# Graph attention edge stage: the gathers leave out rows of the neighbouring node tile

## What is computed

```python
dst = sorted destinations; src = their sources          # 106250 each, 6250 of them self loops
xh    = (layernorm(x) @ W).reshape(N, 8, 32)
a_src, a_dst = einsum(xh, att_src), einsum(xh, att_dst)  # N x 8
e     = leaky_relu(a_src[src] + a_dst[dst])
e     = exp(e - segment_max(e, dst)[dst])
out   = segment_sum(xh[src] * e / segment_sum(e, dst)[dst], dst)
x     = x + batch_norm(out + bias) + layernorm(x)        # then a top-2 mixture of 8 experts, added to x
```

## Time and profile before

| | us |
|---|---|
| median of 3 runs | 1916.98 (1916.75 to 1917.1) |
| span of the profiled execution | 1914.8 |
| that median less that span | 2.2 |
| stage 1 | 0 to 85 |
| edge stage | 85 to about 1200 |
| batch norm, routing, first experts | about 1200 to 1400 |
| experts | 1400 to 1914 |

### The profile page before, as it was taken

One profiled execution on the slowest core, in us unless ns is written; L12 is line 12 of the kernel. 1 busy time (PEld: TensorE's weight loads), 2 busy tenths in 40 slices (PEclk: granted clock), 3 DMA queues, 4 the chain that ended last, 5 costly groups with the idle time before them and its releaser, 6 DMA issues.

```text
span 1914.8 us, 37627 instructions
## 1 busy us (share of the span) xinstructions
PE 1680.9 (88%) x10798; PEld 1177.1 (61%) x10798; DVE 1394.5 (73%) x3802; ACT 1106.1 (58%) x2385; POOL 1216.6 (64%) x1157
## 2 busy tenths in 40 slices
PE   6679898998988989889898888845999999999997
PEld 5445554554545545445454544633989889888896
DVE  6686877877778777787777878897666666666664
ACT  3555676767667666676666765773343443434443
POOL 1377777777777777777777777202556666566653
PEclk9889899999999999998999999977999999999999
DMA  8655446455564555645555444592233323323222
GB/s 282 212 147 145 123 141 166 121 154 158 142 167 119 155 158 142 167 121 154 156 145 163 125 130 113 191 346 103 46 49 50 53 46 55 49 47 54 48 44 35
DMA packets 124146, 240.41 MB, mean 126 GB/s; under 512 B 25064, under 2 KB 82996, under 8 KB 122772
## 3 DMA queue, kind: packets, MB, share of 16 engines
q0 software_dynamic: 62800, 147.76, 32.8%
q1 hardware_dynamic: 51816, 80.51, 12.8%
q10 hardware_dynamic: 9340, 9.73, 1.5%
HBM read 195.47 MB, written 43.30 MB: 125 GB/s over the span
## 4 chain that ended last, share of the span: by engine, by line
PE 44%; POOL 25%; DVE 11%; issue 10%; DMA 7%; ACT 1%; DVEq 1%; POOLq 0%; ACTq 0%; SPq 0%
POOL gather_ring L1115 24%; PE bank L2067 15%; PE bank L2084 14%; PE bank L1240 7%; DMA gather_ring<-node_table,src_slot 4%; PE bank L1206 4%; DVE acc L1139 2%; PE bank L720 1%; PE bank L2048 1%; DVE gather_ring L1167 1%; DVE piece_max L1074 1%; DVE feat L1408 1%; DMA raw_idx<-src_pad,edge_tile_i 1%; ACT r_ring L1392 1%; PE bank L975 1%
## 5 line engine op out<-in xcount | busy, mean ns | idle before, releaser
L1115 POOL DMA_INDIRECT gather_ring<-node_table,src_slot x879 | 838.2, 954 | 268.1 <-issue 254.7
L1206 PE MATMUL bank<-ones 128*128 128x512 bf16 x1787 | 562.0, 395 | 75.4 <-ACT gather_ring L1281 64.1
L1240 PE MATMUL bank<-gather_ring,onehot 128*128 128x264 f32 x1758 | 569.1, 407 | 49.6 <-DVE gather_ring L1167 49.0
L1240 PEld LDWEIGHTS bank<-gather_ring,onehot 128*128 128x128 f32 x1758 | 298.7, 196 | 258.6 <-DVE gather_ring L1167 214.2
L1139 DVE TENSOR_TENSOR acc<-acc,bank 128x264 f32 x879 | 370.4, 421 | 22.7 <-PE bank L1240 21.2
L1167 DVE TENSOR_TENSOR gather_ring<-gather_ring,bank 128x256 f32<-128x256 f32 x879 | 362.1, 412 | 0.3 <-ACT bank L1280 0.3
L2152 POOL DMA_INDIRECT out_rows<-y,token_idx x105 | 201.8, 1922 | 219.6 <-DMA out_rows<-y,token_idx 155.3
L1206 PEld LDWEIGHTS bank<-ones 128*128 128x128 bf16 x1787 | 171.9, 100 | 223.2 <-issue 102.8
L2121 ACT ACTIVATE hid<-bank,cols 128x256 f32<-128x256 f32 (+1 forms) x448 | 209.8, 550 | 141.6 <-PE bank L2067 138.6
L2067 PE MATMUL bank<-xe,w_hi 128*128 128x256 f16 (+1 forms) x1792 | 284.3, 267 | 0.6 <-ACT hid L2121 0.5
L2084 PE MATMUL bank<-w,hid_hi 128*128 x1680 | 278.3, 273 | 0.0
(11 more groups left out here) (315 smaller groups left out, 1963.2 us busy)
## 6 DMA issues: line engine op xcount, KB each, us to landing
w_stage<-in_L_ffn_W SPq DMA_DIRECT2D x16, 1024.0 KB, 7.9
dst_row<-dst_rows SPq DMA_DIRECT2D x110, 128.0 KB, 3.5
gather_ring<-node_table,src_slot POOLq DMA_INDIRECT x879
w_split<-w_out SPq DMA_DIRECT2D x32, 256.0 KB
w<-w_split SPq DMA_DIRECT2D x8, 1024.0 KB, 9.4
node_table<-acc ACTq DMA_DIRECT2D x24, 264.0 KB
r_ring<-in_x_lanes SPq DMA_DIRECT2D x7, 896.0 KB, 6.7
xt<-in_x_lanes SPq DMA_DIRECT2D x24, 256.0 KB, 4.7
```

Source lines behind the costliest of these rows:

```text
L1115: e.indirect_dma_start(out=gather_ring[:, b % GB, j, :], out_offset=None, in_=node_table, in_offset=bass.IndirectOffsetOnAxis(ap=src_slot[ ...
L1206: e.matmul(to[:, :].rearrange("p (k n) -> p k n", k=2), halves[:, 0:P], halves.rearrange("p (a n) -> p a n", a=1).broadcast_to([P, 2, 2 * ...
L1240: e.matmul(bank[AGG[s % len(AGG)]][:, 0:ROW], onehot[:, b % OHB, j, :], gather_ring[:, b % GB, j, :], start=True, stop=True).then_inc(summ ...
```

## The change

The change has three parts.

1. **Order of the lists.** Of each pair, the destination list is fetched and handled first (`which == 0`), then the source list.
2. **Marking rows.** With d the destination less the slot's first node, VectorE computes (d - 127) * d, which is positive only where d lies outside 0 to 127, multiplies it by 8192, and takes the maximum of that and the source index. So a row of another node tile gets an index of at least 1,048,576, and every other row keeps its own. When the transposed list is written, the index is capped at 1,048,576. For the first 32 slots the factor is 0, which leaves their lists whole, because nothing has been written to the ring before them.
3. **Gather with a bound.** Each of the 879 gathers carries the bound 6249, and an index above it is not an error: its row is not fetched and the old content of the buffer stays.

With the given inputs, 6,134 of the 879 * 128 = 112,512 rows are left out (5.45%). They lie in 95 of the 879 gathers, and a gather of these leaves out between 1 and 127 rows. The other 784 gathers fetch what they fetched before.

```diff
+    FAR_SCALE = 8192.0
+    FAR_ROW = FAR_SCALE * P
...
+            e.tensor_scalar(far_first[:, :], part[:, :], float(GB * EB) - 0.5, FAR_SCALE, ALU.is_gt, ALU.mult
+                            ).then_inc(vector_const, 1)
...
-                        out=raw_idx[:, i % 4, :], out_offset=None, in_=(src_pad, dst_pad)[which],
+                        out=raw_idx[:, i % 4, :], out_offset=None, in_=(dst_pad, src_pad)[which],
...
-                if which:
+                if which == 0:
                     e.wait_ge(slot_floats, i + 1)
                     e.wait_ge(slot_keys_made, KEYS_MADE)
-                    e.tensor_scalar(raw_f[:, which, :], raw_f[:, which, :], slot_base[:, g:g + 1], None, ALU.subtract
+                    e.tensor_scalar(raw_f[:, 0, :], raw_f[:, 0, :], slot_base[:, g:g + 1], None, ALU.subtract
                                     ).then_inc(slots_based, 1)
+                else:
+                    e.wait_ge(slots_based, g + 1)
+                    vector_order.of(e.scalar_tensor_tensor(outside[:, :], raw_f[:, 0, :], float(P - 1), raw_f[:, 0, :],
+                                                           ALU.subtract, ALU.mult))
+                    e.wait_ge(vector_order.sem, vector_order.n)
+                    e.wait_ge(slot_floats, i + 1)
+                    e.scalar_tensor_tensor(raw_f[:, 1, :], outside[:, :], far_first[:, 0:1] if g == 0 else FAR_SCALE,
+                                           raw_f[:, 1, :], ALU.mult, ALU.max).then_inc(slots_masked, 1)
...
-                    e.tensor_copy(src_slot[:, g * P:(g + 1) * P], bank[SLOT_TURN[which]][:, 0:P]).then_inc(slots_kept, 1)
+                    e.tensor_single_scalar(src_slot[:, g * P:(g + 1) * P], bank[SLOT_TURN[which]][:, 0:P], FAR_ROW, ALU.min
+                                           ).then_inc(slots_kept, 1)
...
                     if which:
+                        e.wait_ge(slots_masked, i // 2 + 1)
+                    else:
                         e.wait_ge(slots_based, i // 2 + 1)
-                    else:
-                        e.wait_ge(slot_floats, i + 1)
...
                         out=gather_ring[:, b % GB, j, :], out_offset=None, in_=node_table,
-                        in_offset=bass.IndirectOffsetOnAxis(ap=src_slot[:, s:s + 1], axis=0)
+                        in_offset=bass.IndirectOffsetOnAxis(ap=src_slot[:, s:s + 1], axis=0),
+                        bounds_check=N - 1, oob_is_err=False
                     ).then_inc(gathered[b % GB], 16)
```

More of the change, by code:

```diff
@@ L190, in build_gnn_moe @@
         row_up = s1.take("row_up", [P, P])
+        outside = s1.take("outside", [P, P])
+        far_first = s1.take("far_first", [P, 1])
         x_ring = 8
@@ L321, in build_gnn_moe @@
         IOTA_FREE, PART, IOTA_SLOT, TILE_NO, PAD_SRC, PAD_DST, BLANK = range(1, 8)
-        ONES, EPS_MADE, IDENT, ACC_ZERO, PICK_ZERO, MINUS_ONE_UP = range(1, 7)
+        ONES, EPS_MADE, IDENT, ACC_ZERO, PICK_ZERO, MINUS_ONE_UP, FAR_MADE = range(1, 8)
         vector_order = Order(sem("vector_order"))
@@ L351, in build_gnn_moe @@
         SLOT_TURN = (7, 5)
+        slots_masked = sem("slots_masked")
         slots_based, vecs_turned, vecs_kept = sem("slots_based"), sem("vecs_turned"), sem("vecs_kept")
@@ L561, in vector_slot_step @@
             i = n - LISTS_AT - 14
+            if i == 0:
+                e.wait_ge(vector_const, FAR_MADE)
             if 0 <= i < SLOTS_KEPT:
```

## The result

The changed kernel takes 1966.17 us (median of 5 runs, 1964.0 to 1967.12), the kernel before on the same chip 1917.1 us (median of 5, 1916.75 to 1920.08). The ratio is 1.025, with a 95% interval of 1.0239 to 1.026: slower, by 49.1 us. The prediction was 1968.

What follows compares the result with a forecast made beforehand. The prediction took GpSimd's queue of 879 gathers to bound the edge stage. Its terms +1.3 + 0 + 73 - 23 = +51 us gave a forecast of 1968 us, with 1888 to 2130 to hold 8 times in 10.

Steps and rivals of the forecast that it cites:

- What bounds the stage: Edge stage: it costs what 879 gathers cost on GpSimd's queue, 1.25 us each, 1099 us; other engines wait on this pace.
- Part 3, the bound: All 879 gathers: testing each index adds 0.083 us a gather, +73 us, chosen between 0 and +580 us.
- the likeliest case: The forecast itself: a test of 0.01 to 0.25 us a gather, less what is spared; 1922 to 2125 us, chance 0.50.
- What left-out rows spare: Gathers with left-out rows: 6,134 rows at 7.4 ns could give back 0 to 45 us; half taken, -23 us.
- a row left out is a pair spared: Gathers on GpSimd: a left-out row spares its descriptor pair; the faster rival, 1873 to 1896 us with a free test, chance 0.20.
- Part 1, the lists: Stage 1, VectorE's queue: two new list operations a pair, 0.56 us, add +1.3 us, between 0 and 3.9 us.
- Part 2, the register instruction: GpSimd's queue: 879 more instructions are prepared while the previous DMA works and cost 0, upper bound 149 us.
- The bytes: GpSimd's DMA queue: 6.5 MB fewer, about 141.3 MB left if left-out rows are not moved; worth nothing in time.
- The test is free: Rival, gathers: free test and left-out rows spared, 1873 us with full sparing, 1896 with half; chance 0.20.
- nothing changes: Rival, GpSimd: test and sparing cost nothing or cancel within 4 ns a gather, only stage 1 counts, 1918.3 us; chance 0.18.
- The dear form: Rival, gathers: the bounded form costs over +0.25 us a gather, up to +0.66, so 2137 to 2497 us; chance 0.12.

Runs made afterwards that it cites:

- e10: The changed kernel with its bound in a register written once per call of the stage's function, not once per gather: 1964.8 us, ratio 1.0245 to the kernel before.
- e11: The kernel before with only the bound 6249 and its register instructions on every gather, no row left out: 1964.19 us against 1917.81, ratio 1.0242.
- e4: The changed kernel with every index of the gathers after the first 32 marked as outside: 2316.77 us against 2196.44, ratio 1.0506.

## Why the prediction was right, step by step

**What bounds the stage.** Right. 46.2 us more at work in 879 gathers made 46.6 us of the stage, one for one, and in the window every other engine fell back by the same 3 to 4%. One reading was wrong. The prediction took the 10.4 us put down to TensorE for waits that close its sum from 1099 to 1108.8 us. They are 36 idle times of 0.29 us, no longer than the rest and so already in the pitch of 1.25. In their place the difference is the mean gather, 954 ns where the median is 946 (about 6.7 us in all), and 16 reductions of 0.32 us between gathers (5.2 us), less rounding. So nothing could come back when they fell to 2.1 us: "issue" rose from 254.7 to 263.1, and the idle time before gathers is 268.1 us before and 268.5 after. To leave them out of the sum was right, but because they had never been waits.

**Part 3, the bound.** That every gather pays, at the low end, was right; the size was not: +0.052 us measured where I put 0.083, so 46 us instead of 73. The failing step was "work done row by row, with little beside it". The 64-row gathers show 0.8 ns a row where I had at most 7.4, beside 844 ns that by a straight line do not depend on the rows. The scatter that adds misled me: its +0.66 us is a property of that form, and says nothing on how the plain form's time is made up. An eighth of it hit the order of magnitude by choice, not by derivation. Nor do the bounds 1922 and 2125 of the likeliest case follow from its terms: 0.01 us a gather gives 1927 us with nothing spared and 1882 with everything, 0.25 us gives 2138 and 2093.

**What left-out rows spare.** Wrong: I took -23 us, half of the 45 that follow from 7.4 ns a row. It is 0 as far as the traces can tell, at 127 rows out as at 128. My two errors cancel: 73 - 23 = 50 predicted, 46.2 measured. The sum was thus closer than its terms, and it is by luck that the forecast is only 2 us off: with the -23 at its true 0 it would have said 1991 us.

The Trainium skill (DMA: Bandwidth & Descriptors, Anatomy of one DMA) calls descriptor generation "small, variable", with many descriptors to be had before the cost of one more shows. For rows the trace agrees, at 0.8 ns a row beside 844 ns; for the bound it does not give the 52 ns that decide this case. The Trainium skill (DMA: Bandwidth & Descriptors, SWDGE vs HWDGE vs iDMA) has a descriptor pair computed per DMA operation. Read as "a row left out is a pair spared", which I made a rival of, it fell: each left-out row still has its entry in a packet, with 4 bytes.

**Part 1, the lists.** The new operations take what was assumed. VectorE's operations in stage 1 of the changed kernel:

```profile
L584 DVE SCALAR_TENSOR_TENSOR outside<-raw_f 128x128 f32<-128x128 f32 x7 | 2.0, 284 | 0.0
...
L588 DVE SCALAR_TENSOR_TENSOR raw_f<-outside,raw_f 128x128 f32<-128x128 f32 x6 | 1.8, 292 | 0.2
```

And the chain there, against the earlier trace rows:

```profile
58.13 0.22 DVE raw_f L576
58.35 0.26 issue
58.61 6.23 DMA raw_idx<-dst_pad,edge_tile_i
...
66.86 0.33 PE bank L727
67.20 11.34 PE bank L738 x48
```

The fetch in this chain, which the prediction calls the last, is the last but one in both kernels: in the kernel before, GpSimd issues the last one at 59.82, 1.26 us behind the one at 58.56, and it does not hold up the chain. Behind the fetch on the chain the way to the transpose takes 66.86 - (58.61 + 6.23) = 2.02 us where it took 67.46 - (58.56 + 7.00) = 1.90: +0.12, where I had 0.2. Ahead of it I had +1.1 for two pairs. On VectorE's chain a pair of lists takes 2.99 us (52.15 to 55.14) where it took 2.53 (55.49 to 58.02), so +0.46 a pair where I had 0.56. That did not reach the fetch in full: it starts at 58.61, 60.41 and 59.76 us in the three undisturbed traces with the new lists (the changed kernel twice, and e10), and at 58.56 and 58.84 in the two with the old ones (the kernel before, and e11), so between 0 and +1.8. Against this the fetch itself is shorter with the new lists (6.23, 6.55 and 6.31 us for 7.00 and 6.95), of which I have no explanation that was tried. In the end the first gather starts at 84.9, 87.0 and 86.1 us with the new lists and at 85.3 and 86.8 with the old ones. The +1.3 us can be neither confirmed nor refuted by these; it is below the scatter of the stage.

**Part 2, the register instruction.** Right in its sum, 0, and in the main in its reason: the instruction is dealt with ahead of its gather. I had it under the DMA just ahead; in the trace it runs 10 to 12 gathers earlier. What I did not see is that it moves the batch's wait off the gather. It costs nothing here because those gathers hide the wait. Where none are lined up, a gather starts 0.50 us later than with the wait on itself.

**The bytes.** Right: q0 has 141.30 MB, as worked out. They are worth nothing, and e4 showed that even 114 MB are not.

**The rivals.** "The test is free" and "nothing changes" needed a test under 51 ns and a change within 4.4 ns per gather. The first fell mainly because nothing is spared, the second on the 52 ns. The dear form (+0.25 us and more) did not appear, in neither mode of the bound.

No version that beats the kernel before came out of this. By the straight line a gather costs 844 ns before its first row, and 0.30 us of idle time, so fewer gathers with more rows each would be the way to speed up this stage. That was not tried: the gathers of this kernel take one index per partition, and all 128 are in use.

## What to carry to other kernels

Where a queue issues one indirect DMA after another, first ask how much of an issue's time depends on its rows, and measure it by halving the rows: here 0.8 of 946 ns per row, so that leaving out 6,134 rows could have given back 5 us at most, before any detail of the change was looked at. The bound on such a DMA is paid at every issue (52 ns times 879), while the rows it is for were in 95 of them. Before you call idle time a wait, compare its length with that of the idle time beside it: here 36 "waits for TensorE" were as long as no wait at all. When a forecast comes out right, check its terms one by one: here two wrong ones of opposite sign stood behind a sum that was only 2 us off.

## What the runs showed of the hardware

- An indirect gather of 128 rows takes GpSimd 946 ns, one of 64 rows 895. With a bound it is 998 and 937, and 1013 (128 rows) in the mode that treats an index beyond it as an error. How many rows are really beyond the bound, none, 127 or 128, changes nothing.
- A row left out by the bound is still moved as a 4-byte element: a packet of four such rows has 16 bytes, and the number of packets stays the same.
- GpSimd's queue handles a register instruction 10 to 12 gathers (15.9 us at the median) ahead of its own gather, when nothing makes it wait.
- When no gather is lined up, a gather whose wait stands on the register instruction just ahead of it starts 0.78 us after what it waited for ended, and 0.28 us when the wait stands on the gather itself.
- Three chips ran the unchanged kernel in 2176 to 2196 us, where it takes 1917 to 1918 in the other runs. Without a bound the gathers took the same 946 to 949 ns there.
